# Routed experts in rounds of two pairs, four gather buffers, and a reordered first and last group, in a two-layer token kernel on one core

## What is computed

```python
x = x + _L0_ffn_ref(_L0_cond_ref(x, itok_B_0_7, L0_cond_weights, fside_8xS_0), L0_ffn_gate_w, ...)
x = x + _L1_ffn_ref(_L1_cond_ref(x, L1_cond_W, L1_cond_A, L1_cond_Bm, L1_cond_scalings, itok_B_0_6), ...)
```

```python
scores = jax.nn.softmax((xt @ gate_w.T).astype(jnp.float32), axis=-1)
top_w, top_idx = jax.lax.top_k(scores, TOP_K)
for e in range(E):
    h = jax.nn.silu(xt @ w1[e].T) * (xt @ w3[e].T)
    y = y + dense_w[:, e:e + 1] * (h @ w2[e].T)
z = jax.nn.silu(xt @ sw1.T) * (xt @ sw3.T) @ sw2.T
```

## Time and profile before

| | us |
|---|---|
| median of 3 runs (422.18 to 422.45) | 422.25 |
| the profiled execution | 423.68 |
| its span, first to last instruction | 421.9 |
| TensorE busy | 410.9 (97%) |
| VectorE busy | 306.9 (73%) |
| ScalarE busy | 248.1 (59%) |
| GpSimd busy | 190.5 (45%) |

### The profile page before, as it was taken

How to read it: one execution, slowest core, us unless ns; L and a number is a source line. 1 busy time by engine, 2 the same in 40 slices (tenths; PEclk the granted TensorE clock), 3 DMA queues, 4 the chain that set the end, 5 groups by cost and what they waited for, 6 DMA issues and landing times.

```text
span 421.9 us, 8675 instructions
## 1 busy us (share of the span) xinstructions
PE 410.9 (97%) x2947; PEld 332.0 (79%) x2947; DVE 306.9 (73%) x732; ACT 248.1 (59%) x552; POOL 190.5 (45%) x195
## 2 busy tenths in 40 slices
PE   7999999999899999999999999999999999999996
PEld 5668788888799999999999998885675755757553
DVE  6987978998966766765665654859678686786844
ACT  3996566574355665565556554238567485674854
POOL 4420079502544544454454305637575585755020
PEclk9999999999999999999999999999999999999999
DMA  8999200000255555555555623312232242322111
GB/s 243 373 385 363 69 0 2 0 2 16 64 179 176 157 159 161 168 162 161 157 173 159 132 76 99 87 52 66 85 101 87 64 122 83 98 87 64 50 51 51
DMA packets 37274, 50.44 MB, mean 120 GB/s; under 512 B 4488, under 2 KB 30480, under 8 KB 37232
## 3 DMA queue, kind: packets, MB, share of 16 engines
q1 hardware_dynamic: 30032, 31.89, 22.4%
q0 software_dynamic: 6480, 17.70, 15.5%
q10 hardware_dynamic: 720, 0.30, 0.3%
HBM read 32.18 MB, written 17.69 MB: 118 GB/s over the span
## 4 chain that ended last, share of the span: by engine, by line
PE 83%; DVE 7%; ACT 5%; DMA 2%; issue 1%; POOL 1%; ACTq 0%; DVEq 0%
PE bank L1153 17%; PE bank L1155 16%; PE bank L1154 16%; PE bank L1428 13%; PE bank L1443 6%; PE bank L1317 4%; PE bank L1355 2%; PE bank L1356 2%; PE bank L1337 2%; ACT xtr L471 2%; PE bank L1394 2%; ACT xtT L485 2%; DMA xres<-in_x 1%; DVE hsl L783 1%; DVE hsf L776 1%
## 5 line engine op out<-in xcount | busy, mean ns | idle before, releaser
L408 POOL DMA_INDIRECT xg<-kept,perm x71 | 69.0, 971 | 90.8 <-PE bank L1317 56.3
L1428 PE MATMUL bank<-h,wg 128*128 128x512 fp8e4 x256 | 61.7, 380 | 0.2 <-ACT ff L651 0.2
L1153 PE MATMUL bank<-w13h,xgl 128*128 x142 | 48.8, 344 | 0.2 <-issue 0.2
L1428 PEld LDWEIGHTS bank<-h,wg 128*128 128x128 fp8e4 x256 | 22.2, 98 | 33.9 <-ACT ff L651 12.8
L984 DVE TENSOR_TENSOR hrl<-bank,hrh 128x256 fp32r<-128x256 f32 (+1 forms) x36 | 15.1, 420 | 45.0 <-issue 34.1
L415 POOL DMA_INDIRECT ga<-slots_out,slot x32 | 32.1, 1004 | 33.9 <-SPq L353 17.3
L1155 PE MATMUL bank<-w13h,xgh 128*128 x142 | 45.8, 322 | 0.0
L1154 PE MATMUL bank<-w13l,xgh 128*128 x142 | 45.7, 322 | 0.0
L649 ACT ACTIVATE gel<-bank 128x512 bf16<-128x512 f32 x64 | 40.3, 630 | 6.4 <-PE bank L1428 3.2
L415 POOL DMA_INDIRECT gb<-slots_out,slot x32 | 37.8, 1182 | 9.8 <-issue 9.8
L651 ACT ACTIVATE ff<-bank 128x512 bf16<-128x512 f32 x64 | 40.9, 638 | 0.0
(11 more groups left out here) (198 smaller groups left out, 1160.0 us busy)
## 6 DMA issues: line engine op xcount, KB each, us to landing
slots_out<-yr SPq DMA_DIRECT2D x35, 256.0 KB
xres<-in_x SPq DMA_DIRECT2D x7, 512.0 KB, 9.0
kept<-xtr SPq DMA_DIRECT2D x7, 512.0 KB, 8.6
out_x<-fin SPq DMA_DIRECT2D x7, 512.0 KB
w13raw<-in_rw SPq DMA_DIRECT2D x8, 352.0 KB, 5.2
w2raw<-in_rw SPq DMA_DIRECT2D x8, 256.0 KB, 6.5
wgst<-in_wgate SPq DMA_DIRECT2D x16, 128.0 KB
xg<-kept,perm POOLq DMA_INDIRECT x71
```

The source lines that it names most:

```text
L408: pool.indirect_dma_start(out=xg[:, i % 2, j, :], out_offset=None, in_=kept, in_offset=bass.IndirectOffsetOnAxis(perm[:, 2 * i + j:2 * i + ...
L1153: pe.matmul(dst, al, bh, start=first, stop=False, skip_group_check=True)
L1428: ins = pe.matmul(bank[bk][:, :], wg8[:, kk, half, c * P:(c + 1) * P], h8[:, k, kk, :], start=(kk == 0), stop=(kk == KC - 1))
```

## The change

- **Routed stage.** After a hand-written start, the pairs are taken two at a time. A round n (even) is, on TensorE, `routed_hT` of pairs n-2 and n-1, `routed_T` of pairs n+2 and n+3, then up(n), down(n-2), up(n+1), down(n-1). VectorE and ScalarE follow the same rounds. `hr`, `hrh`, `hrl` are doubled; the short transposed part of pair i goes into bank 4 or 7 beside its long part.
- **Gathers.** Four `xg` buffers in other memory, so a gather waits for the transposes of four pairs earlier. The staging of the second layer's weights shrinks to two steps.
- **First stage.** The first group's tokens come in one DMA on SP's queue; a few more `ones`; `shared_up(0)`'s first part stands ahead of the last gate products and of `logits(0)`; `shifted(0)` moves behind `routed_weight_lo(0)` on VectorE. Of the splits of expert weights, those of 2 and 3 come earlier.
- **Second layer.** In every group `linear(g + 1, 1)` and `adapters_up(g + 1)` stand ahead of the last three chunks of the first half of `ffn_down`. Of group 6's second half only two chunks stay ahead of the last group; the other six stand between the last group's up products. Its eviction and POOL's addition come behind the last group's products. `last_down` computes three tiles chunk by chunk.

```diff
-            for n in range(1, PAIRS):
-                if n + 1 < PAIRS:
-                    routed_T(n + 1, (n + 1) % 2)
-                routed_hT(n - 1, n == 1)
-                routed_up(n, n % 2, experts[n])
-                if n % 4 == 3 and n + 1 < PAIRS:
-                    experts += experts_of((n + 1) // 4)
-                routed_down(n - 1, (n - 1) % 2, experts[n - 1], n <= 2)
+            routed_T(2, 0)
+            routed_hT(0)
+            routed_up(1, 1, experts[1])
+            routed_down(0, 0, experts[0], True)
+            routed_T(3, 1)
+            routed_hT(1)
+            routed_up(2, 0, experts[2])
+            routed_T(4, 0)
+            routed_T(5, 1)
+            routed_up(3, 1, experts[3])
+            experts += experts_of(1)
+            routed_down(1, 1, experts[1], True)
+            for n in range(4, PAIRS, 2):
+                routed_hT(n - 2)
+                routed_hT(n - 1)
+                for i in range(n + 2, min(n + 4, PAIRS)):
+                    routed_T(i, i % 2)
+                routed_up(n, 0, experts[n])
+                routed_down(n - 2, 0, experts[n - 2])
+                routed_up(n + 1, 1, experts[n + 1])
...
+                routed_down(n - 1, 1, experts[n - 1])
+            routed_hT(PAIRS - 2)
             routed_hT(PAIRS - 1)
             shared_up(EARLY, parts=[0])
+            routed_down(PAIRS - 2, 0, experts[PAIRS - 2])
             routed_down(PAIRS - 1, 1, experts[PAIRS - 1])
```

On VectorE, and ScalarE's counterpart (`routed_h_hi` twice, silu, `routed_x_hi`, y, silu, `routed_x_hi`, y, and `second_hi` twice where n < 8):

```diff
+            for n in range(4, PAIRS, 2):
+                routed_h_lo(n - 2)
+                routed_h_lo(n - 1)
+                routed_mul(n)
+                if n + 2 < PAIRS:
+                    routed_x_lo(n + 2, 0)
+                routed_mul(n + 1)
+                if n + 2 < PAIRS:
+                    routed_x_lo(n + 3, 1)
+                if n < 2 + 2 * W_STEPS:
+                    cast_step((n - 2) // 2)
+                if n < 4 + 2 * L1_PARTS:
+                    second_lo((n - 4) // 2)
```

POOL's gathers and its last addition, the first DMA, and the last groups:

```diff
-                if i >= 2:
-                    pool.wait_ge(s("xr_T"), i - 1)
+                if i >= GATHERS:
+                    pool.wait_ge(s("xr_T"), i - GATHERS + 1)
...
+                    if g == GROUPS - 2 and h:
+                        pool.wait_ge(s("act8_ready"), GROUPS * HC)
...
-            sp.dma_start(xres[:, 0:2, :], x_t[0][:, 0:2, :]).then_inc(x_first[0], 16)
+            sp.dma_start(xres[:, 0:GT, :], x_t[0]).then_inc(x_in[0], 16)
...
                     ffn_up(g, k, c, first)
+                    if last and c + SPREAD < HC:
+                        ffn_down(g - 1, 1, first, [c + SPREAD])
...
-                ffn_down(g, 0, first, range(5, HC))
                 linear(g + 1, 1)
                 adapters_up(g + 1)
-                ffn_down(g, 1, first)
+                ffn_down(g, 0, first, range(5, HC))
+                if g + 2 < GROUPS:
+                    ffn_down(g, 1, first)
+                    return
+                for c in range(SPREAD):
+                    ffn_down(g, 1, first, [c])
```

More of the change, by code:

```diff
@@ L271, in adaln_ffn @@
                      "comb_a comb_done xm_T xm_hi xm_split xa_done xa_m xa_hi xa_split H_done h8_ready "
-                     "gate_done up2_done gel_ready ff1_ready act_ready act8_ready down_done ob_ready fin_ready last_ready").split():
+                     "gate_done up2_done gel_ready ff1_ready act_ready act8_ready down_done act8_used ob_ready fin_ready last_ready").split():
             s(name)
-        x_first = [sem(f"x_first{h}") for h in range(2)]
         x_in = [sem(f"x_in{g}") for g in range(GROUPS)]
@@ L278, in adaln_ffn @@
         kept_late = sem("kept_late")
-        xg_in = [sem(f"xg_in{k}") for k in range(2)]
+        xg_in = [sem(f"xg_in{k}") for k in range(GATHERS)]
         y_out = [sem(f"y_out{k}") for k in range(2)]
@@ L604, in _ @@
             routed_silu(0)
-            def routed(i, k, first=False):
-                routed_h_hi(i - 1)
-                routed_x_hi(i + 1, k)
-                routed_silu(i)
-                routed_y(i - 1, k, first)
             def second_hi(q):
@@ L616, in second_hi @@
                 act.activation(l1h[:, q, :], l1st[:, q, :], ACT.Copy).then_inc(s("l1_hi"), 1)
-            for i in range(1, PAIRS - 1):
-                routed(i, (i + 1) % 2, i <= 2)
-                if 4 <= i < 4 + L1_PARTS:
-                    second_hi(i - 4)
+            routed_h_hi(0)
+            routed_x_hi(2, 0)
+            routed_silu(1)
+            routed_y(0, 0, True)
+            routed_h_hi(1)
+            routed_x_hi(3, 1)
+            routed_silu(2)
+            routed_x_hi(4, 0)
+            routed_silu(3)
+            routed_x_hi(5, 1)
+            routed_y(1, 1, True)
+            for n in range(4, PAIRS, 2):
+                routed_h_hi(n - 2)
+                routed_h_hi(n - 1)
+                routed_silu(n)
+                if n + 2 < PAIRS:
+                    routed_x_hi(n + 2, 0)
+                routed_y(n - 2, 0)
+                routed_silu(n + 1)
+                if n + 2 < PAIRS:
+                    routed_x_hi(n + 3, 1)
+                routed_y(n - 1, 1)
+                if n < 4 + L1_PARTS:
+                    second_hi(n - 4)
+                    second_hi(n - 3)
             routed_h_hi(PAIRS - 2)
-            routed_silu(PAIRS - 1)
+            routed_h_hi(PAIRS - 1)
             routed_y(PAIRS - 2, 0)
-            routed_h_hi(PAIRS - 1)
             routed_y(PAIRS - 1, 1)
@@ L679, in ffn @@
                 down_out(g, 0, first)
-                down_out(g, 1, first)
+                if g + 2 < GROUPS:
+                    down_out(g, 1, first)
             x_hi(0, True)
@@ L995, in _ @@
             routed_x_lo(1, 1)
-            link(dve.tensor_scalar(hr[:, 2, :], ident[:, 0:P], 0.0, None, ALU.mult))
+            for k in range(2):
+                link(dve.tensor_scalar(hr[:, k, 2, :], ident[:, 0:P], 0.0, None, ALU.mult))
             routed_mul(0)
@@ L1447, in ffn_down @@
                     ins.then_inc(s("down_done"), 1)
+                elif len(chunks) == 1:
+                    ins.then_inc(s("act8_used"), 1)
             shared_up(EARLY, parts=range(1, 6))
```

156 lines of the change are left out of this document (85 added, 71 removed).

## The result

The changed kernel takes 427.01 us (median of 4 runs, 426.93 to 428.47) where the kernel before takes 422.22 beside it: a ratio of 1.0121, 95% interval 1.0108 to 1.0135. That is 4.8 us slower. The sign of the forecast was right, its size was not: 424.3, 2.1 slower, was predicted, less than half of what came. The profiled execution took 426.95 with a span of 425.1.

The account below looks back on a forecast made before the run. The prediction took TensorE's matmuls to bound the routed stage. Its terms, savings outside the rounds against losses in the new rounds and written-out start, summed to +2.1 us on the median 422.25, giving 424.3, range 419.3 to 427.5.

Parts of the forecast that it names:

- The baseline: Whole kernel: the sum of +2.1 us, made in a profiled execution of 423.68, was applied to the median of 422.25.
- First stage and VectorE's waits: Before the first up product: earlier tokens and clock rise -0.7 us, one expert's split fewer in VectorE's way -0.6.
- Start of the routed stage: First pairs: shorter waits for VectorE, pair 2's gather (0.38) and a late silu (0.4), together -1.4 us.
- The late silu: Pair 1, start of routed stage: ScalarE's unexplained 2.05 us wait until 120.17 might go; 0.4 us taken as gain.
- written-out start: Hand-written first pairs: up(3) has only two pairs' transposes between itself and up(2), one set awaiting a split; +1.0 us.
- The new place in a round: Second up products of each round: a 1.45 us chain against 1.35 of down products, 0.2 us lost a round, +3.4.
- The second layer's copies: First two rounds: ScalarE's two extra copies push the splits and the multiplication, 0.4 us each, +0.8.
- Transposes in one run: Routed stage on TensorE: fourteen transposes in a run save changes between transposes and products, -0.1 us, 0.3 at most.
- VectorE: Rival for the rounds: two pairs' splits end after silu and delay the multiplication, 0.45 us a round, 428; chance 0.10.
- They can end about 0.4 before it is due: Each round on VectorE: both pairs' splits, 2.0 us, finish about 0.4 us before the multiplication is due.
- End of the stage: Last routed pair: part of `shared_up` now stands between up(35) and down(35), removing a wait, -0.45 us.
- Last group: Second layer's end: moved products bring the last eviction earlier, but group 6's store gives much back; -0.45 us.

Follow-up runs that it names:

- before_again: The kernel before, unchanged, profiled once more: 422.95 us, span 421.1.
- gath_only2: Kernel before with only four gather buffers and the smaller staging of weights, second run: ratio 1.0002.
- front_last: Kernel before with the changed first stage, linear and adapters moved, and three last tiles chunk by chunk: 421.40 us, ratio 0.9980.
- front_only: Kernel before with the changed first stage alone: ratio 0.9989.
- mulfirst2: Changed kernel with VectorE's multiplication of pair n between the two splits instead of behind both, second run: 426.77 us, ratio 1.0087.
- cover_T: Changed kernel with the four transposes of pair n+3 moved from the start of a round to its middle: 425.93 us, ratio 1.0103.
- cover_mul2: Changed kernel with pair n+3's transposes in the middle of the round and VectorE's multiplication between the splits, second run: 423.13 us, ratio 1.0018.
- old_tail: Changed kernel with its last group as before, linear and adapters keeping their new place: 427.32 us, ratio 1.0134.
- best2: Changed kernel with middle transposes, multiplication between splits and group 6 as before, last three tiles still chunk by chunk, second run: 422.30 us, ratio 1.0003.
- tail_only: Kernel before with the changed second layer alone: ratio 1.0007.
- mulfirst: Changed kernel with VectorE's multiplication of pair n between the two splits instead of behind both, first run: 441.5 us.
- tail_nowait: Changed kernel without the wait that holds GpSimd's last addition until the last group's last cast, first run: 442.6 us.
- cover_mul: Changed kernel with pair n+3's transposes in the middle of the round and VectorE's multiplication between the splits, first run: 432.5 us.
- best1: Changed kernel with middle transposes, multiplication between splits and group 6 as before, last three tiles still chunk by chunk, first run: 431.7 us.
- gath_only: Kernel before with only four gather buffers and the smaller staging of weights, first run: 426.6 us, ratio 1.0065.

## Why the prediction was right or wrong

**The baseline** was the first failed step: "It is made in the profiled execution ..., which is 1.4 above the median of the runs; I apply it to the median". Gains were counted in things that the usual execution does not have. The late silu ("I find no cause for it"), credited with 0.4, is absent from before_again and gath_only2. The pair of 3.88, which the round of 7.77 rests on, is 3.86 in before_again, front_last and gath_only2: the changed round loses 0.24 and not 0.20 against the usual kernel. The profile stood 1.4 above the median, and a sum of what the change takes from that profile was applied to the median. From profile to profile the change is 425.1 - 421.9 = 3.2; from median to median 4.8.

**First stage and VectorE's waits** (-0.7 and -0.6 by up(0)): -1.37 in the trace of after, 1.4 in front_only. Right, and the clock had a part in it: the granted clock rose to its upper level at 6.2 us instead of 12.3, and group 0's transposes took 1.09 instead of 1.92. It can be lost again. In mulfirst2 TensorE stood idle for 3.4 us before its second group of mixing products, the clock was at the lower level from 10.6 to 14.0 us, those transposes took 1.97, and up(0) came at 113.61, later than before; in the other traces with this first stage it came at 111.4 to 112.3.

**Start of the routed stage.** Gather -0.38, silu -0.4, written-out start +1.0, together +0.2: measured +0.5. The difference is about the size of the silu's term, which had nothing to give back. Pair 5's gather brought a new wait of 0.61 before its transposes, against the forecast's "no wait for a gather".

**The new place in a round** (+3.4, a chain of 1.45 us against 1.35 of cover): the mechanism and its size were right (16 rounds at 0.2 are 3.2, though, not 3.4). The last up product of pair n started at 177.52, the multiplication ended at 178.64 (1.12, as forecast), up(n+1) came 0.35 later (0.33), 0.11 late (0.10), with 0.26 to its successor. cover_T took the wait away where it should, and cover_mul2 gave 4.7 us back. **The second layer's copies** (+0.8): 2 x 0.45 = 0.9. Right.

**Transposes in one run** (-0.1): not there. From the last transpose to the first up product and on to the second are 0.27 us after the fourteen and 0.27 us after the seven of before, which is what one transpose (0.11) and one up product (0.16) take anyway. There was nothing to gain. cover_mul2 has no such wait in its rounds up to n = 30 and takes 7.76 for two pairs, 0.04 more than 2 x 3.86. Some 0.03 of that is in the 22 products of every second pair, whose starts are a few ns further apart, as they are in the pairs of 3.89. Why is open.

**VectorE** was a rival for all rounds with 0.10. It holds none of the ordinary ones, but all of the three in which ScalarE's copies push the splits (counted) or in which no transposes of `xg` stand between `routed_hT` and the up products. The last is n = 34. "They can end about 0.4 before it is due" was a wrong reading even of an ordinary round. There the splits ended at 177.74, the multiplication of the first tile began at once (177.77), and that of the second, which waited for silu, followed at 178.23: the slack was some 0.03. The last round has no `routed_T`, 0.88 us of TensorE's work less ahead of up(n), and it lost 0.7. That was not seen.

**End of the stage** (-0.45, and two ordinary rounds with +0.4): +1.0 of like work. The forecast had no term for the last round's VectorE wait of 0.7. mulfirst2, without VectorE's wait, has 46.57 there, 0.2 more than before_again in like work; with the 0.4 of its two rounds in it, the removed wait gave some 0.2 back and not 0.45.

**Last group** (-0.45): +0.7 from group 6 on, and -0.1 in the groups before. The step that failed is the end of its chain. TensorE's last product did come earlier, 27.73 behind group 6's first instead of 28.97, and the addition and the store started where forecast (415.5 and 416.6, with 2.57 taken off). But the sum stopped when the last data had moved. Counted from group 6's start, the stores were in only 0.15 earlier than before (SyncE's wait ends at 421.30 against 421.45, with 2.57 taken off), and then came the barrier. From TensorE's last product to the end it was 4.02 and is 5.96: SyncE's wait for the stores 0.9 longer, the closing barrier 0.8 longer, the issues 0.2 longer. So the gain of 1.24 was given back 1.6-fold. What the runs show of the reasons is in the last section.

**Sum.** With before_again, its late tokens taken off (up(0) at 112.84), as the usual execution: -1.4 + 0.2 + 4.0 + 1.5 - 0.1 + 0.7 = +4.9 in the table's columns, against 4.8 in the medians. The forecast's misses against it are, of like work, about 0.7 in the rounds (mostly the baseline), 1.0 at the end of the stage, 1.0 in the last groups and 0.3 at the start.

## What to carry to other kernels

Take a second profile of the kernel before, or set the first beside the median, before counting a wait as something to gain: a stall without a cause in the trace may be that execution's, or that chip's, and not the kernel's. Where an order puts one engine's work for two items in a row, check the rounds at the edges of the loop, in which the other engine's filler is missing, and not only the steady one. Carry the chain of the last result through the last store's landing and the closing barrier; the last matmul is not the end.

## What the runs showed of the hardware that was not expected

**A load of instructions among the last stores.** From group 6's first product to the end before, before_again and gath_only2 took 32.99 to 33.06, while front_only, with the same tail, took 33.65 with TensorE's last product at the same distance (28.97). The view of DMAs shows what differs. front_only, from the first of the last issues on (the first is at 416.41), in 40 slices of 0.09 us:

```profile
GB/s 0 0 0 0 0 0 0 0 0 0 296 353 375 398 353 341 364 387 364 376 387 273 69 23 193 353 364 364 171 34 23 23 23 11 0 0 0 0 0 0
...
q14 instruction: 1, 0.01, 1.0%
```

before_again, from the same point on (417.92), in slices of 0.08 us:

```profile
GB/s 0 0 0 0 0 0 0 0 0 0 0 66 277 330 423 370 410 383 383 357 410 357 396 383 357 384 397 383 396 238 66 0 0 0 0 0 0 0 0 0
```

There is a hole in the stores (69, 23 GB/s), and one packet of the instruction queue in this stretch (at 417.33), where before_again had its packet ahead of the first issue (at 417.51). The three issues took 1.67 instead of 1.39 and the wait behind them 1.7 instead of 1.4, 0.6 in all. old_tail, front_last and best2 had the packet 0.9 to 1.0 us behind the first issue too, with issues of 1.65 to 1.81 and waits of 1.7. tail_only, the new tail with the packet ahead of the three issues, took 33.36 where the changed kernel took 33.69. So part of what looked like the cost of the new tail depends on where a block of instructions ends. That the load causes the hole is argued from its place, not shown. In the changed kernel the packet comes at the end of the issues, and why TensorE's sequencer reaches the barrier 0.8 later there stays open.

**A hold on some chips.** The experiments ran on five chips. On two of them (before at 423.65 and 423.85, elsewhere 422.0 to 422.5) five kernels, all with four gather buffers, took 4.6 to 15.7 us longer than the same kernel on another chip (432.5 against 423.1, 441.5 against 426.8, 442.6 against 426.8, 431.7 against 422.3, 426.6 against 422.0). In all of them but the last, ScalarE and GpSimd waited up to 3.0 us at a time with no releaser that the profile can name (`remote`), though the products of TensorE that they needed had long started.

The waits go with gathers that follow one another without a pause. mulfirst and tail_nowait issue four in a row in every round, and from 141 us on ScalarE stood for 2.0 to 2.9 us in each of twelve rounds. cover_mul and best1, on the same two chips, issue two at a time there; they were held only at the start, while 12 gathers ran in a row, and their rounds take 7.76. Two buffers show a small form of it, behind five gathers in a row: 4.67, 5.05 and, in the first profile, 4.80 from pair 1 to pair 2 instead of 3.86. That the gathers cause it is argued from this, not shown, and on the other chips the same runs of gathers cost nothing. It is a risk of long runs of gathers that the median of one chip does not show.

Part of the loss is the clock's. In mulfirst TensorE was idle for 5.3 us, and the granted clock was 0.50, the lower level, from about 118 to 124.4 us; the twelve up products of pair 1 stand 0.29 us apart instead of 0.16, some 1.6 us together. cover_mul, tail_nowait and best1 show the same, gath_only, whose wait was shorter, does not.
